# An octonion feed-forward kernel: the 85-row leftover chunk of Down filled to 128 rows by copies inside the chip, with new unit orders

## The reference, cut to what matters

```
S_OCT[8, 8, 8]                                   # signs of the octonion product
Wq = scale * clip(round(W / scale), -1, 1)       # scale = mean |W|, ternary weights
M  = einsum('jik,jod->koid', S_OCT, Wq)
linear(x, W) = einsum('...id,koid->...ko', x, M)  # x in 8 components
x  [1, 2048, 1024];  w_gate, w_up [8, 341, 128];  w_down [8, 128, 341]
xn  = (x - mean) / sqrt(var + 1e-5)
h   = silu(linear(xn, w_gate)) * linear(xn, w_up)     # 8 components of 341
out = x + autocorrelation_part(xn) + linear(h, w_down)
```

## Time and profile before

| | |
|---|---|
| median of 3 runs | 573.12 us (572.56 to 573.49) |
| the profiled execution | 571.62 us |
| its span (first to last instruction) | 569.8 us |
| matmuls | 6852, mean granted clock 0.997 |
| busy share of PE, DVE, ACT, POOL | 97%, 83%, 67%, 82% |
| HBM read, written | 21.23 MB, 8.39 MB |

### The profile page before, as it was taken

How to read it: one execution, slowest core, us unless ns; L and a number is a source line. 1 busy time by engine, 2 the same in 40 slices (tenths; PEclk the granted TensorE clock), 3 DMA queues, 4 the chain that set the end, 5 groups by cost and what they waited for, 6 DMA issues and landing times.

```text
span 569.8 us, 16765 instructions
## 1 busy us (share of the span) xinstructions
PE 554.2 (97%) x6852; PEld 523.7 (92%) x6852; DVE 471.2 (83%) x1227; ACT 384.0 (67%) x620; POOL 465.7 (82%) x335
## 2 busy tenths in 40 slices
PE   5999998999989999999999999999999999999998
PEld 5899997899979999999999999999999999999997
DVE  3887999796968879888789879888889879975965
ACT  4878889965875478845986578745985484645430
POOL 3407649898997989899989988998989987999950
PEclk9999999999998999999999999999999999999999
DMA  6620202001220031200320040100320021102022
GB/s 185 203 76 1 75 2 77 1 1 40 112 75 1 3 108 43 76 2 28 123 75 2 2 141 18 68 3 38 112 76 2 2 75 39 39 2 76 2 76 77
DMA packets 12072, 30.70 MB, mean 54 GB/s; under 512 B 906, under 2 KB 5850, under 8 KB 11994
## 3 DMA queue, kind: packets, MB, share of 16 engines
q1 hardware_dynamic: 11994, 29.62, 15.2%
HBM read 21.23 MB, written 8.39 MB: 52 GB/s over the span
## 4 chain that ended last, share of the span: by engine, by line
PE 73%; POOL 13%; issue 8%; DVE 2%; DMA 2%; ACT 1%; SPq 0%; POOLq 0%; ACTq 0%; DVEq 0%
PE acc L548 26%; PE acc L416 15%; PE acc L409 14%; PE acc L426 10%; POOL hop L1859 4%; PE acc L465 4%; POOL hs L1852 2%; POOL hs L1847 2%; POOL hs L1851 2%; PE acc L482 2%; DMA hop<-in_w_gate 2%; PE acc L439 2%; POOL hs L1846 1%; POOL hop L1856 1%; PE acc L495 1%
## 5 line engine op out<-in xcount | busy, mean ns | idle before, releaser
L548 PE MATMUL acc<-wd,hop 128*128 128x128 f16 (+1 forms) x2944 | 169.9, 219 | 0.0
L548 PEld LDWEIGHTS acc<-wd,hop 128*128 128x128 f16 (+1 forms) x2944 | 166.8, 98 | 0.4
L832 ACT ACTIVATE pk<-acc 128x512 f32<-128x512 f32 (+1 forms) x120 | 66.6, 556 | 79.5 <-PE acc L426 30.5
L1856 POOL TENSOR_TENSOR hop<-hx,hop 128x1024 f16<-128x1024 f32 (+1 forms) x46 | 98.2, 2134 | 7.3 <-ACT hop L900 7.3
L1859 POOL TENSOR_TENSOR hop<-hs,hop 128x1024 f16<-128x1024 f32 (+1 forms) x46 | 98.2, 2135 | 6.8 <-ACT hop L910 6.3
L1846 POOL TENSOR_TENSOR hs<-hx 128x512 f32<-128x512 f32 (+1 forms) x47 | 60.3, 1283 | 35.4 <-DVE hx L1417 23.7
L426 PE MATMUL acc<-wl,xop 128*128 128x172 f16 x1024 | 84.1, 239 | 1.8 <-DVE hx L1423 1.6
L426 PEld LDWEIGHTS acc<-wl,xop 128*128 128x128 f16 x1024 | 78.6, 98 | 3.5 <-DVE hx L1423 2.1
L1306 DVE TENSOR_TENSOR bd<-acc,pk 128x256 f32<-128x256 f32 (+1 forms) x104 | 40.4, 389 | 48.9 <-ACT pk L832 48.8
L1851 POOL TENSOR_TENSOR hs<-hs 128x512 f32<-128x512 f32 (+1 forms) x47 | 59.8, 1273 | 3.7
L1852 POOL TENSOR_TENSOR hs<-hs 128x512 f32<-128x512 f32 (+1 forms) x47 | 60.4, 1285 | 0.0
(11 more groups left out here) (199 smaller groups left out, 1062.3 us busy)
## 6 DMA issues: line engine op xcount, KB each, us to landing
xr<-in_x SPq DMA_DIRECT2D x16, 512.0 KB, 4.2
zx<-in_x SPq DMA_DIRECT2D x16, 512.0 KB, 3.6
out_y<-zx SPq DMA_DIRECT2D x15, 512.0 KB, 2.6
hop<-in_w_down SPq DMA_DIRECT2D x1, 1364.0 KB, 10.9
hop<-in_w_gate SPq DMA_DIRECT2D x2, 512.0 KB, 7.3
hop<-in_w_up SPq DMA_DIRECT2D x1, 1024.0 KB
hop<-in_w_gate SPq DMA_DIRECT2D x1, 340.0 KB
hop<-in_w_up SPq DMA_DIRECT2D x1, 340.0 KB
```

Source lines behind the costliest of these rows:

```text
L548: last = nc.tensor.matmul(dst, operand(g, c, t, form, level), wd[0:WIDE[c], slot, c, :], start=which == 0 and c == CHUNKS[0] and s // 2 no ...
L832: nc.scalar.activation(pk[:, q % 2, :, 0:wide], pair[:, :, T:T + wide], ACT.Copy, scale=XS if u[0] == "X" else 1.0).then_inc(copied, 1)
L1856: nc.gpsimd.tensor_tensor(half_of(g, c, 4 * Y, 1), by_tile(h), half_of(g, c, 4 * Y, 0), ALU.subtract).then_inc(h_free, 1)
```

## The change

**Down.** For chunk 2 the 43 rows above 85 that were empty are filled. BOTH = 43 and TAIL = 42. The low rows 0 to 42 of a form are copied beneath its 85 high rows (to rows 85 to 127 of level 0), and the same is done once with the weights in `wd`. The low rows 43 to 84 of a form go beneath the 85 low rows of another form, its host. `pairs` lists 16 pairs of table rows that add to the same quarter; for each there are now three matmuls: the first form's full column, the second form's, and one of 127 rows with both tails, against a new weight tile `wtail` (one block of 128 columns per pair), whose rows 0 to 42 are zero. Before there were four. The layout of `hop` becomes level before form, so that four forms of a level lie together.

**Copies.** SP issues 34 DMAs for the weights (2 within `wd`, 32 from `wd` to `wtail`) after the first loads of `zx`, and 12 per leftover h unit, 24 per group, from `hop` to `hop` (`stack`), between its loads and stores. The first half of Down waits at chunk 2 for all 24 of its group and for the weights. POOL sets `wtail`'s rows 0 to 42 to zero in the opening.

**Orders.** SECOND, STEADY and FINAL and the lists of ACT and DVE are new. `power(g)` moves on POOL from behind the second turned unit of a group to its middle, `refine` on ACT from the start of a group to the end of the one before, `fold_sum` becomes a step of its own on DVE, and four small tiles become parts of others.

```diff
+    BOTH = P - REST
+    TAIL = REST - BOTH
+    HOST = {0: 6, 6: 3, 3: 4, 4: 2, 2: 7, 7: 0, 1: 5, 5: 1, **{f: f + 4 for f in range(8, 12)}, 12: 11, 13: 10, 14: 9, 15: 8}
...
-    SECOND = ("F' L00' *F' L01' G00 +L00' L11' +L01' L10' +G00 H0' +L11' L01 +L10' G01 H1' U00 +L01 +G01 L10 L00 +U00 L11 "
-              "+L10 X0 +L00 G10 +L11 N0 H0 +G10 U01 +N0 +U01 H1 G11 X1 N1 +G11 U10 U11 +N1")
-    STEADY = ("+U10' G01 +U11' G00 U01 +G01 L00 +G00 U00 +U01 L01 +L00 L10 +U00 L11 +L01 N0 +L10 G11 X0 +L11 +N0 +G11 H0 H1 "
-              "F' G10 *F' X1 N1 +G10 U10 U11 +N1")
-    FINAL = ("+U10' L11 +U11' G01 G00 +L11 U01 +G01 L10 +G00 U00 +U01 L01 +L10 N0 +U00 +L01 H1 L00 G11 +N0 +L00 +G11 F' H0 "
-             "G10 *F' U10 U11 N1 +G10 +U10 +U11 +N1")
+    SECOND = ("L00' F' L01' L10' +L00' *F' +L01' L01 L11' +L10' H0' +L01 L00 +L11' G00 H1' U00 +L00 +G00 G01 L10 +U00 G10 "
+              "+G01 X0 +L10 L11 +G10 N0 +L11 H0 U01 X1 +N0 +U01 G11 H1 N1 +G11 U10 U11 +N1")
+    STEADY = ("+U10' G01 +U11' G00 L00 U01 +G01 +G00 U00 +L00 L01 +U01 L10 +U00 +L01 L11 N0 +L10 G11 +L11 X0 +N0 +G11 H0 H1 "
+              "F' G10 X1 N1 *F' +G10 U10 U11 +N1")
+    FINAL = ("+U10' +U11' L10 G01 G00 U00 +L10 +G01 U01 L01 +G00 +U00 L11 +U01 +L01 G10 N0 +L11 +G10 L00 +N0 H1 +L00 F' *F' "
+             "H0 G11 U10 U11 N1 +U10 +G11 +U11 +N1")
...
-    power_at = {h_no[0, 1, 0]: 2}
-    power_before = {max(h_no[g - 2, 2, 0], h_no[g - 2, 2, 1]) + 1: g for g in range(3, G)}
+    power_at = {h_no[0, 1, 0]: 2, **{max(h_no[g - 2, 2, 0], h_no[g - 2, 2, 1]): g for g in range(3, G)}}
...
+            for rows in (slice(0, BOTH - 1), slice(BOTH - 1, BOTH)):
+                sp.dma_start(wd[REST + rows.start:REST + rows.stop, :, 2, :], wd[rows, :, 2, :]).then_inc(w_stacked, 16)
+            for k, (_, _, _, slot, _, guest_slot, _) in enumerate(pairs):
+                sp.dma_start(wtail[BOTH:REST, k, :], wd[BOTH:REST, slot, 2, :]).then_inc(w_stacked, 16)
+                sp.dma_start(wtail[REST:REST + TAIL, k, :], wd[BOTH:REST, guest_slot, 2, :]).then_inc(w_stacked, 16)
+
+            def stack(g, Y):
+
+                sp.wait_ge(h_ready, h_no[g, 2, Y] + 1)
+                a, b = halves[g, 2]
+                for first in (4 * Y, NJ + 4 * Y):
+                    for rows in (slice(0, BOTH - 1), slice(BOTH - 1, BOTH)):
+                        sp.dma_start(hop[REST + rows.start:REST + rows.stop, a:b + 1:b - a, 0, first:first + 4, :],
+                                     hop[rows, a:b + 1:b - a, 1, first:first + 4, :]).then_inc(stacked[g % 2], 16)
+                    for f in range(first, first + 4):
+                        sp.dma_start(hop[REST:REST + TAIL, a:b + 1:b - a, 1, HOST[f], :],
+                                     hop[BOTH:REST, a:b + 1:b - a, 1, f, :]).then_inc(stacked[g % 2], 16)
...
+                    if c == 2:
+                        if which == 0:
+                            pe.wait_ge(tail_zero, 1)
+                            pe.wait_ge(w_stacked, 16 * (2 + 2 * len(pairs)))
+                            pe.wait_ge(stacked[g % 2], 16 * 24 * (g // 2 + 1))
+                        for k, (kind, Y, s, slot, form, guest_slot, guest) in enumerate(pairs):
...
+                            for lhs, rhs in ((hop[:, half, 0, form, :], wd[:, slot, c, :]), (hop[:, half, 0, guest, :], wd[:, guest_slot, c, :]),
+                                             (hop[0:REST + TAIL, half, 1, form, :], wtail[0:REST + TAIL, k, :])):
...
+            nc.gpsimd.memset(wtail[0:BOTH, :, :], 0.0).then_inc(tail_zero, 1)
```

More of the change, by code:

```diff
@@ L51, in octonion_ffn_attention_kernel @@
     NS, NSD = 24, 26
+    BOTH = P - REST
+    TAIL = REST - BOTH
+    HOST = {0: 6, 6: 3, 3: 4, 4: 2, 2: 7, 7: 0, 1: 5, 5: 1, **{f: f + 4 for f in range(8, 12)}, 12: 11, 13: 10, 14: 9, 15: 8}
+    pairs = []
+    for which, table in enumerate((DOWN_SPECTRAL, DOWN_TERMS)):
+        for Y in range(2):
+            for s in range(4):
+                two = [(slot, form) for q, slot, form in table[Y] if q == s]
+                (guest_slot, guest), (slot, form) = two if HOST[two[0][1]] == two[1][1] else two[::-1]
+                pairs.append((which, Y, s, slot, form, guest_slot, guest))
     DIRECTS = 2
@@ L189, in octonion_ffn_attention_kernel @@
         vr = sb("vr", [P, NTILE], F32)
[L190 to L193, removed]
+        twos = sb("twos", [P, 4 * NT], F32)
+        r0, hv, rr, mh = [twos[:, NT * i:NT * i + NT] for i in range(4)]
+        one_half = few[:, 23:24]
         rs = sb("rs", [P, NTILE], F32)
@@ L264, in operand @@
                 return xop[rows, G % 2, form, level, P * t:P * (t + 1)]
-            return hop[rows, halves[g, c][t], form, level, :]
+            return hop[rows, halves[g, c][t], level, form, :]
         def dot_room(g, t):
@@ L277, in half_of @@
             a, b = halves[g, c]
-            return hop[0:WIDE[c], a:b + 1:b - a, first:first + 4, level, :]
+            return hop[0:WIDE[c], a:b + 1:b - a, level, first:first + 4, :]
         def by_tile(a):
@@ new lines, in sooner @@
+            def sooner(g):
+                return (0, 1) if h_no[g, 2, 0] < h_no[g, 2, 1] else (1, 0)
+            for Y in sooner(0):
+                stack(0, Y)
+            load_x(3)
+            store(0, 0)
+            stack(1, sooner(1)[0])
+            store(0, 1)
+            for g in range(2, G - 1):
+                stack(g - 1, sooner(g - 1)[1])
+                store(g - 1, 0)
+                if g + 2 < G:
+                    load_x(g + 2)
+                stack(g, sooner(g)[0])
+                store(g - 1, 1)
@@ L349, in _ @@
+            stack(G - 2, sooner(G - 2)[1])
+            store(G - 2, 0)
+            for Y in sooner(G - 1):
+                stack(G - 1, Y)
+            store(G - 2, 1)
+            for t in range(NT):
+                store(G - 1, t)
             sp.wait_ge(out_st, 16 * NTILE + 32)
@@ L542, in down @@
                             pe.wait_ge(tail_ready, t + 1)
+                    if c == 2:
[4 more added lines that the diff above has]
+                        for k, (kind, Y, s, slot, form, guest_slot, guest) in enumerate(pairs):
+                            if kind != which or s // 2 not in banks or s not in spots:
+                                continue
+                            at = T * (s % 2) + P * Y
+                            dst = last_quarter[:, at:at + P] if spots == (0,) else acc[:, bank[n], s // 2, at:at + P]
+                            half = halves[g, c][t]
+                            for lhs, rhs in ((hop[:, half, 0, form, :], wd[:, slot, c, :]), (hop[:, half, 0, guest, :], wd[:, guest_slot, c, :]),
+                                             (hop[0:REST + TAIL, half, 1, form, :], wtail[0:REST + TAIL, k, :])):
+                                last = nc.tensor.matmul(dst, lhs, rhs, start=which == 0 and c == CHUNKS[0] and s // 2 not in seen, stop=False,
+                                                        skip_group_check=which == 1)
+                                seen.add(s // 2)
+                        continue
                     for Y in range(2):
@@ L992, in second_group @@
-                normalise(2, 1)
[L993 to L1001, removed]
-                base(("N", 0, 0))
-                odd_two(("G", 1, 0, 1))
-                eights(("T", 1, 1))
-                base(("N", 0, 1))
@@ L1403, in x_adds @@
                 first_adds(u)
+                if u[2] == 1:
+                    fold_sum(u)
                 second_adds(u)
```

333 lines of the change are left out of this document (172 added, 161 removed).

## The result

| | before | changed |
|---|---|---|
| median of 4 runs each, same chip | 572.84 us (571.71 to 573.49) | 583.92 us (583.26 to 584.74) |
| ratio | | 1.0196, 95% interval 1.0178 to 1.0213 |
| span of the profiled execution | 569.8 us | 581.6 us |
| matmuls | 6852 | 6596 |
| mean granted clock | 0.997 | 0.979 |

What follows compares the result with a forecast made beforehand. PE was taken to bound groups 2 to 7, with POOL close behind, and POOL group 1. Terms -14.3 - 4.1 - 2.0 + 2.6 + 3.3 + 1.7 = -12.8 gave span 557.0, median 560.3 us; 8-in-10 range 554.5 to 567.

Steps and rivals of the forecast that it cites:

- The copies at the first Down: First Down, chunk 2: PE waits 2.2 us for the last copies plus some clock loss, +2.6 us (0 to 7).
- rival C: First Down: small copies slower than their issue back up the queue, wait 58x - 38, kernel slower than before; chance 0.06.
- The argument against it: Against slow copies: 3.03 MB in packets of 1 KB kept 59 ns a packet.
- The end: FINAL and last Down: PE waits for ACT's power and the tail's late low levels, +1.7 us (0 to 4).
- The wait for ACT's power: In FINAL, where *F' follows F' directly, PE waits about 0.7 us.
- the one for POOL's low levels: Last Down: the tail's low levels come about 1 us late, as Down shortens and the h chain doesn't.
- Copies in the steady groups cost nothing: Steady groups: copies cost PE nothing, SP issuing by 236 us and N0 coming at 251.4, a cover of 13 us.
- Fewer matmuls: Down's leftover chunk: 256 fewer matmuls at 55.8 ns each, -14.3 us.
- The wait at 170 us: PE's 2.4 us wait at 168 to 170 us and 1.7 us of clock loss behind it go, -4.1 us.
- PE's waits in group 1: Group 1: of 3.0 us of PE's other waits about 1 us stays, -2.0 us (-3 to 0).
- Steady groups: Groups 2 to 6: POOL with waits of 2.1 and 1.7 us makes 62.3 us a group, +3.3 us (0 to 6).
- The memset: POOL's zeroing of wtail in the opening takes 2 to 4 us within idle time, 0 us (0 to 0.5).

Runs made afterwards that it cites:

- both ends plain: Changed kernel with groups 0 and 7 back to four matmuls for the leftover chunk, groups 1 to 6 keeping three and their copies: 564.50 us, ratio 0.986.
- the orders alone: Changed kernel's new unit orders with four matmuls in every group and no copies on SP: 572.67 us, ratio 1.000 to the kernel before.
- the last base swapped: New orders, four matmuls everywhere, no copies, and ACT writes the very last tile's base after the pk step instead of ahead: 569.12 us, ratio 0.9951.

## Why the prediction was wrong, step by step

- **The copies at the first Down** (+2.6, 0 to 7): 15.3 us, and this is the step that failed. Its term "SP needs 0.81 us for two issues, so 0.4 each" carried a DRAM load's issue over to copies inside SBUF of 42 rows, which took 0.79 to 0.87. With 0.84 the prediction's own formula in rival C, 58x - 38, gives 10.7; SP began 2.3 us later than taken, at 88.1. The rival had the right place, the right sum and nearly the right deciding point (0.9 us per copy), and too low a chance, 0.06. Its reason was another one: there each copy was to take longer than its issue, while here the issue itself was long and a block landed 1.3 us behind its last one. The argument against it spoke of transport, 59 ns a packet, which the same bytes in 11 DMAs show to be no part of the matter.
- **The end** (+1.7, 0 to 4): 9.0 us. Of these 7.8 are the copies. The prediction did not ask for the cover of the last 12 as it had for the others: PE comes for them 6.3 us after POOL's last leftover step (546.0 to 552.3), and they need 1.0 us for the queue to come free, 9.9 to be issued and 1.3 to land. The wait for ACT's power came as forecast, 0.84 us for 0.7; the one for POOL's low levels, about 1 us, did not come, and with both ends plain PE doesn't wait for POOL there either. A wait for DVE adds 0.4.
- **Copies in the steady groups cost nothing**: right. PE waited for them at the two ends only. A block took 10 us to issue, where 4.9 had been taken, and the cover was enough: in the group that starts at 212 us the last copy was issued by 254.7, and PE came to chunk 2 at 263.2.
- **Fewer matmuls** (-14.3): the count is right, the price 51 ns and not 55.8. A half takes 4.95 us where it took 5.36; 32 halves give -13.1. The 24 matmuls of the leftover chunk take 57.5 ns each.
- **The wait at 170 us** (-4.1): gone with its clock, but 1.4 us of smaller waits for DVE and ACT stand in the same group.
- **PE's waits in group 1** (-2.0): 1.55 us idle from 82 us to the wait, 3.0 before, so -1.5.
- **Steady groups** (62.3 us each): 62.28, with POOL's two waits where they were forecast and about as long, 58.5 + 2.1 + 1.6. But it doesn't follow that POOL with these waits is the bound: with the first of them gone the group stayed as long. PE's sum gives the same number, 61.6 (63.28 less 4 x 0.41) plus 0.6 of waiting at H1 for DVE, where the prediction had PE late at U11 through ACT. So the number was right with a cause that isn't shown, and in part by luck.
- **The memset**: 1.94 us, and POOL still waited 1.84 us behind it. Nothing.
- **The opening**: not in the prediction; PE is 1.2 us later by 19 us, from a granted clock of 0.57 between 12 and 16 us. In that stretch the three profiles of kernels with the opening of before show 1.00; of the eleven with the changed opening two show 1.00 and nine 0.50 to 0.79, and kernels with the same opening stand on both sides (the orders alone 1.00, with the last base swapped 0.57). Whether the change makes the low clock likelier stays open; no run here was made for it.

From the forecast's -12.8 to +11.8 of span these make 12.7 + 7.3 + 1.2 + 1.4 + 0.5 + 1.2 = 24.3 of the 24.6 us.

## What to carry to other kernels

Price a small DMA by the issue time of its own kind, and multiply by the count before thinking of bytes; then ask at each place where it is used, first and last ones above all, what work covers the whole queue ahead of it. A stage in the middle may hide copies that both ends pay for in full, and there the older, dearer form can be kept: here 64 of the 256 matmuls, given back, brought 19 us. And a wait on a busy engine doesn't make it the bound: shorten the wait, and see whether the period moves or only another wait grows. If it doesn't move, follow the waits once around the period before calling another engine the bound; the way may close over several engines.

## What the runs showed of the hardware

An issue on SP took 0.38 to 0.43 us from DRAM. Inside SBUF it took 0.56 to 0.60 for 1, 16, 32, 43, 48, 64, 80 and 128 rows, and 0.73 to 0.79 for 40, 42, 44, 45 and 84. With 42 rows it was the same for 512 bytes and 2 KB a row, and a second piece per row added 0.08. 43 rows landed after 3.75 us, 42 after 1.2. Behind each long wait of PE the granted clock stood at the 1.2 GHz level and was back at 2.4 GHz by 142.2 and 562.1 us; over nearly 5 us of work it was 0.59 and 0.60 on the mean, so a wait of 5.9 us and one of 13.4 cost the same 1.9 us more.
